# Unused bf16 products added to TensorE's work per chunk in two stages of a two-layer graph network

## The reference

```
h = relu(layernorm(x))
# layer 0: mlp(h, W) = batchnorm(relu(h @ W + b)) over all rows
node_feat = mlp(h, W_node)
edge_feat = mlp(edge_attr, W_edge)
message   = mlp(concat(h[row], h[col], edge_feat), W_msg)
x = x + segment_sum(message, col) + node_feat
# layer 1
h = relu(layernorm(x))
features = gcn_conv(h, W_gcn)        # segment_sum(h[src] * norm)
x = x + h + relu(features @ W1 + b1) @ W2 + b2
```

## Time and profile before

| what | value |
|---|---|
| median of three runs | 6323.46 us (6308.38 to 6337.69) |
| profiled execution, its own time | 6340.04 us |
| its span | 6337.5 us |
| its mean granted clock of PE | 0.763 |
| PE busy (products) | 5203.0 us, 82% |
| PE weight loads busy | 3460.6 us, 55% |
| VectorE busy | 4202.3 us, 66% |
| ScalarE busy | 4829.9 us, 76% |
| GpSimd busy | 3254.9 us, 51% |

### The profile page before, as it was taken

One profiled execution on the slowest core, in us unless ns is written; L12 is line 12 of the kernel. 1 busy time (PEld: TensorE's weight loads), 2 busy tenths in 40 slices (PEclk: granted clock), 3 DMA queues, 4 the chain that ended last, 5 costly groups with the idle time before them and its releaser, 6 DMA issues. The chain is left out here.

```text
span 6337.5 us, 128256 instructions
## 1 busy us (share of the span) xinstructions
PE 5203.0 (82%) x34818; PEld 3460.6 (55%) x34818; DVE 4202.3 (66%) x13257; ACT 4829.9 (76%) x11024; POOL 3254.9 (51%) x3411
## 2 busy tenths in 40 slices
PE   6755548888788888888788888787669999999998
PEld 5411115555455555555555555554437777777777
DVE  5577775555555555555555555555449999999996
ACT  3566647778777777777777777777339999999996
POOL 3577757777777777777777777777310000000000
PEclk7555557777876687776877667778559999999998
DMA  4444433433433333343333333433111111111121
GB/s 155 139 124 123 123 87 94 113 93 96 114 94 113 93 94 111 93 112 91 94 112 94 108 96 93 114 94 96 55 53 63 63 63 73 74 63 63 63 77 71
DMA packets 329554, 593.56 MB, mean 94 GB/s; under 512 B 142708, under 2 KB 199044, under 8 KB 316692
## 3 DMA queue, kind: packets, MB, share of 16 engines
q1 hardware_dynamic: 216868, 329.75, 16.5%
q0 software_dynamic: 103344, 158.83, 11.6%
q10 hardware_dynamic: 8640, 96.77, 4.0%
HBM read 430.51 MB, written 154.44 MB: 92 GB/s over the span
## 5 line engine op out<-in xcount | busy, mean ns | idle before, releaser
L978 POOL DMA_INDIRECT gbuf<-a_tab,idxb x2688 | 2596.4, 966 | 927.2 <-issue 793.6
L1888 ACT ACTIVATE nf<-psum 128x600 bf16<-128x600 f32 x2604 | 1522.4, 760 | 12.2 <-PE psum L1879 5.4
L1078 DVE TENSOR_TENSOR pre<-psum,gbuf 128x384 f32<-128x384 f32 x806 | 449.6, 558 | 1395.6 <-PE psum L1065 1192.2
L1065 PE MATMUL psum<-rhs,lhs 128*128 128x96 f32 x6448 | 1192.1, 345 | 0.1
L1879 PE MATMUL psum<-x_all 128*128 128x300 bf16 x5208 | 1071.7, 292 | 76.5 <-DVE x_all L1872 31.6
L1065 PEld LDWEIGHTS psum<-rhs,lhs 128*128 128x128 f32 x6448 | 1066.4, 250 | 106.2 <-issue 60.2
L1871 DVE TENSOR_SCALAR x_all<-x_all,dstrel 128x600 bf16<-128x600 f16 x2604 | 966.3, 371 | 100.6 <-PE psum L1879 11.0
L1109 PE MATMUL psum<-msg,oh 128*128 128x388 f32 x1612 | 981.5, 703 | 0.0
L1119 ACT ACTIVATE x_all<-psum 32x97 f32<-32x97 f32 x3224 | 782.5, 243 | 132.7 <-PE psum L1129 93.4
L1197 ACT ACTIVATE x_all<-psum 128x300 bf16<-128x300 f32 x1260 | 524.3, 416 | 386.4 <-PE psum L1186 385.1
L1901 PE MATMUL psum<-x_all,nf 128*128 128x96 bf16 x12400 | 805.1, 205 | 1.2 <-issue 0.6
(11 more groups left out here) (231 smaller groups left out, 6332.0 us busy)
## 6 DMA issues: line engine op xcount, KB each, us to landing
adj_tab<-x_all ACTq DMA_DIRECT2D x60, 1575.0 KB
gbuf<-a_tab,idxb POOLq DMA_INDIRECT x3224
x_all<-dst_row SPq DMA_DIRECT2D x806, 64.0 KB
x_all<-adj_tab SPq DMA_DIRECT2D x30, 1575.0 KB, 6.5
x_all<-attr_parts SPq DMA_DIRECT2D x807, 36.0 KB
x_all<-attr_parts SPq DMA_DIRECT2D x403, 72.0 KB
spilled<-gbuf SPq DMA_DIRECT2D x134, 192.0 KB, 1.9
gbuf<-spilled SPq DMA_DIRECT2D x134, 192.0 KB
```

Source lines behind the costliest of these rows:

```text
L978: g.indirect_dma_start(gbuf[:, k % 4, t, :], None, a_tab[:, :], bass.IndirectOffsetOnAxis(ap=idxb[:, k % 4, t:t + 1], axis=0)).then_inc(g_ ...
L1065: ins = pe.matmul(ps_m(k)[:, t, :], lhs[:, k % 2, t * TILE:(t + 1) * TILE], rhs[:, k % 2, :], start=True, stop=True)
L1888: act.activation(adj[:, w % 2, :, j * SLOT:(j + 1) * SLOT].rearrange("p (b h) s -> p b h s", b=2), ps_a(n).rearrange("p b (h s) -> p b h s ...
```

## The change

Two calls of a new helper are added. In the node stage PE makes eight more bf16 products of 128 columns per chunk, between the wide product with `wnode` and the eight f32 products with `wab`. In the stage between the layers it makes four more bf16 products of 256 columns per chunk, ahead of the wide product with `wc`. Weights and moving operand are both the identity's bytes read as bf16; each product also loads its 128x128 weights. The results go to unused columns of a PSUM bank and nobody reads them. No wait and no semaphore is added or removed.

```diff
+        def keep_warm(pe, unused, n):
+
+            pe.matmul(unused, ident[:, :].bitcast(BF16)[:, 0:P], ident[:, :].bitcast(BF16)[:, 0:n], start=True, stop=True)
+
 ...
             pe.wait_ge(n_a.sem, n_a.at(c - 2))
             pe.wait_ge(n_b.sem, n_b.at(c - 2))
+            for _ in range(8):
+                keep_warm(pe, bank[4 + k % 2][:, CT * C:CT * C + P], P)
             for t in range(CT):
                 rows = every(lhs[0:C, k % 2, :], t)
 ...
             pe.wait_ge(p_t.sem, p_t.at(c - 2))
+            for _ in range(4):
+                keep_warm(pe, bank[6 + k][:, CT * H:CT * H + 2 * P], 2 * P)
             pe.matmul(bank[4 + k][0:H + 1, :], wc[:, :], u_cols[k], start=True, stop=True)
```

## The result

Slower by 0.7%: 6372.14 us, the median of six runs (6357.53 to 6382.47), against 6330.62 for the kernel before in six runs (6308.38 to 6337.69). The ratio is 1.0069, 95% interval 1.0057 to 1.0081. The forecast was +37.5 us, the difference of the medians is +41.5. The profiled execution has a span of 6369.2 us, 31.7 more than before.

The account below looks back on a forecast made before the run. PE was taken to bound the node stage, and one loop with a PE stop the stage between the layers. Terms of 17 + 20.5 = +37.5 us moved the median from 6323.46 to 6361 us, range 6328 to 6388.

Parts of the forecast that it names:

- PE sets the node stage and nothing covers the added products: Node stage: PE has no gap, so added products lengthen each chunk from 6.06 to 6.72 us, the stage by 17 us.
- The share of clock-bound work at the high level: Node stage: share of clock-bound work done at the high clock rises from 11 to 20%, of 1.69 us per chunk.
- The rise between the layers: Stage between the layers: occasional clock rises give back 1 us of the 21.5 us price, leaving +20.5 us.
- The stop of 2.17 us does not cover the added products: Between the layers: the four products don't use PE's standstill before L1555; 25 x 0.86 = 21.5 us at the low level.
- Added weight loads are free: Both stages: each added product's weight load hides behind the product before it, so nothing is added for loads.
- Rival A: Both stages: added products hold the clock high; node -17, between the layers -23, total -40 us, 6283; chance 0.05.
- B: The clock holds high in the node stage alone: -17 + 21.5 = +4.5 us, 6328; chance 0.12.
- Rival C: Both stages: the clock gives nothing back; +25.5 node, +21.5 between the layers, total +47 us, 6370; chance 0.20.
- rival D: Both stages: added products hidden or cheaper, 0.45 us per chunk, rest as now; +22.5 us, 6346; chance 0.06.
- Recorded busy time alone does not hold the clock: Node stage, against the skill's rule: from 95 to 115 us PE was busy 20.00 of 20 us, yet granted 0.51.

Follow-up runs that it names:

- e6_fill_8: Kernel before plus eight unused 256-column products per round in PE's stop between the layers, from chunk 5 on; that stage 264.2 us (before 264.3).
- e4_between16: Kernel before plus sixteen unused 128-column products per node-stage chunk, two ahead of each narrow product; node stage 168.3 us (before 160.6).
- e10_best: Kernel before plus four 512-column products per node-stage chunk, ahead of every second narrow product, and twenty 256-column ones in the between-layers stop; 6290.51 us against 6336.3.
- e7_between8: Kernel before plus eight unused 128-column products per node-stage chunk, one ahead of each narrow product; node stage 189.7 us (kernel before 161 to 162 on that chip).
- e9_between8_256: Kernel before plus eight unused 256-column products per node-stage chunk, one ahead of each narrow product; node stage 153.6 us (before 160.6).

## Why the prediction was right

The sign, the size and the places came out. Two of its terms were off, in opposite directions: the node stage by +3.4 us, the stage between the layers by -6.9. That the sum came so near is in part luck: the two stages gave 34.0 us, the medians 41.5, and the message stage scatters by more than these differences.

- PE sets the node stage and nothing covers the added products: right, each chunk grew. The stage gained 20.4 us where 17 were forecast.
- The share of clock-bound work at the high level: mis-sized. The forecast took 20% after 11%, that is 0.20 x 1.69 = 0.34 us back per chunk; the old work had none of it. The forecast saw that a rise comes when the dense part is nearly over, but let it vary from chunk to chunk. In fact the longer chunk fell into step with the clock, and each rise hurried only the added group (0.48 us instead of 0.86), 0.38 us back, so that the wrong share cost the sum almost nothing, by luck. By what rule the clock rises and falls these runs do not show.
- The rise between the layers: mis-sized. 1 us was taken back, the trace gives 21.5 - 13.6 = 7.9. By the distances about half comes from three pairs of neighbouring rounds with the wide product at or partly at the high level (9.03 and 9.57 to 9.65 us instead of 9.92), the other half from the last steps, which have no stop. The forecast had named these steps and still priced them as the others.
- The stop of 2.17 us does not cover the added products: right, since they stand behind L1561, and `e6_fill_8` shows that 1.7 us of such work ahead of it is free.
- Added weight loads are free: right within the row (`L439` eight in 0.48 us), wrong at its end. The narrow group, forecast at 3.64 us as before, took 3.79, since its first weight load no longer ran beside the wide product. This is the term that made the chunk 6.20 + 0.48 + 0.15 = 6.83 us in place of 6.72. Between f32 narrow products each added product costs 0.08 us at the high level and 0.14 at the low one.
- Rival A and B, that the clock holds, failed in the change for the reason given against them: the run of narrow products let it fall. `e4_between16` and `e10_best` show the positive: with products between the narrow ones the clock stays at 1.00 and transposes and wide product halve. Rival C came true for the node stage's old work only, and rival D's price of 0.45 us for its added work only; 20.4 us lie between C's 25.5 and D's 11.3.
- Recorded busy time alone does not hold the clock: in `e7_between8` PE was recorded busy for 33.00 us of 33, and the clock was 0.50. The advice of the Trainium skill ("TensorE: Matmul & The Clock Gate", section "Why this matters for your kernels") to keep TensorE continuously busy is not enough here; what held the clock in `e9_between8_256` and `e10_best` were products put where PE waited for weight loads.

## What to carry to other kernels

Work added to raise TensorE's clock pays only if the high level lies over work that is bound by columns; look in the timeline which groups change their duration with the clock and which don't, before counting on a higher mean. Put such work where TensorE waits anyway, in a stop for another engine or beside long weight loads, with many columns per weight load (512 were the most tried), and enough of it to hold the level through the sparse part; in line with dense work, behind it (+21.5 us) or ahead of it (+6.3 us net), it lengthened the stage. Judge it by stage lengths from the trace when the rest of the kernel scatters by more than the effect.

## What was not expected of the hardware

- A loop of TensorE work and its clock can fall into step: 22 chunks in a row of 6.83 us, with the same groups at the low level each time; from another start the distances ran towards the same 6.83. Doubling the added work in that place cost nothing more (180.4 against 182.1 us), and moving the eight ahead of the transposes gave 166.9.
- A product with 32 weight columns on PSUM partitions 96 to 127 between products with 128 weight columns cost 0.57 us (two distances of narrow groups 2.07 us, against 0.467 each), its own weight load 0.10 us long: the loads before and after it stopped overlapping.
- Between f32 products with their own weights an added bf16 product costs 0.078 us at the high level whether it streams 128 or 256 columns (0.545 against 0.467 us), and 0.14 with 128 columns at the low one (0.605).
